# Last layer of a four-layer transformer kernel: up products in another order, one stored down product behind each, and the bias of four batches moved ahead

## The chip, the cores and the metric

The kernel runs on one core of one Trainium2 chip. The metric is the device time of one execution in microseconds (us); lower is better. TensorE does the matrix products (in the profile PE, and PEld for its weight loads), VectorE is DVE, ScalarE is ACT, GpSimd is POOL, and SyncE (SP) issues most of the DMAs.

## What is computed

The reference runs four layers one after the other on x [16, 256, 256] with context [16, 256, 256]. Each is x = x + layer(layernorm(x)): an attention whose keys are picked by an argmax, a top-2 mixture of experts, a cross attention with 16 heads of 64, and last the one that the change touches:

```python
grouped = x.reshape(b, s // 32, 32, d)          # 128 groups of 32 tokens, d = 256
logits = einsum('bntd,des->bntes', grouped, Wc) + bc + tie
perm = (logits == max over the 32 tokens)        # one token for each of 128 units (e, s)
permuted = einsum('bntd,bntes->bnesd', grouped, perm)
inner = relu(einsum('bnesd,esdf->bnesf', permuted, W1) + b1)       # f = 32
result_permuted = einsum('bnesf,esdf->bnesd', inner, W2) + b2
result = einsum('bnesd,bntes->bntd', result_permuted, perm)
```

So each of 128 units has small weights W1 [256, 32] and W2 [32, 256] of its own ("up" and "down"), applied to one picked token of each of 128 groups. b2 is added by unit and carried back to the tokens by perm.

## The kernel before, in words

Every engine has one instruction stream, written out by hand for all layers; semaphores (`w.wait_ge`) order them. The order on an engine is the order of the calls in the code, so an instruction that waits holds up all that stands behind it on its engine. The last layer consists of two parts.

**Steps** (`pe_step`, `dve_step`, `act_step`, `pool_step`, n from 0 to 19). They run over the 16 batches of 256 tokens, pipelined: at step n TensorE turns the choice of batch n-2 (L1765), computes the logits of n-1 (L1773), turns batch n (L1781) and gathers the picked tokens of n-3 (`gather`, L1799: 32 matmuls into the four banks GATHER). ACT and DVE copy the gathered tokens to `PX` (L2063, L1947). GATHER holds 64 groups after batch 7 and 64 more after batch 15. At n = 11 the four up products of the first half of the groups (batches 0 to 7, called "a" below) are made by `pe_up(…, 0, j)` (L1830, 64 matmuls, which the profile shows as 128 pairs of weight load and matmul, since one fp32 matmul is issued as two), each for a quarter j of the units, and DVE adds b1 and takes the relu (`dve_up`, L1998 and L2005).

**Tail** (`pe_tail`, `dve_tail`, `act_tail`, `pool_tail`, `sp_tail`). On TensorE:

- `pe_up(…, 1, x)`, x = 0 to 3: the up products of the second half of the groups ("b"), quarter j = PARTS[1][x]; results go to `INY[j]`, W1 comes from the buffers `WF1P`, two of which (2 and 3) lie where `RPA[1]`, `WF2P[2]` and `R2A` are placed later.
- `down_a(k)`, k = 0 to 7 (L1855, 16 matmuls, 32 pairs): down product of half a, for eight units in each half of them. DVE and ACT copy it to one of two buffers `RPA[k % 2]` (`take_a`, L2026 and L2074, two copies each). SP and POOL each store half of the buffer (512 KB each) to DRAM, `rp_scratch` (L2161, L2116). `take_a(k)` waits until the store of k-2 has ended (`rpa_free`). W2 comes in four quarters `WF2P[k // 2]` of 1024 KB; quarter 2 can only be loaded after the last up product, quarter 3 only after `down_b(1)`, and both loads (`second`, L2125) stand on SP's queue behind stores.
- `down_b(k)` (L1872, 16 matmuls, 32 pairs): the same for half b, copied to `RPB` in SBUF (L2038 and L2084). It uses the GATHER banks, and each waits until the copies of the one before it are done.
- The order was a0, up, up, up, a1, up, a2, b0, a3, b1, a4, b2, a5, b3, a6, b4, a7, b5, b6, b7. `done_a(k)` and `done_b(k)` are the counts of the semaphore s_fm that go with it.
- The last loop, i = 0 to 9: `turn_b(i)` (L1884, 16 transposes of `RPB`, to which DVE adds b2, L2048), `bias(i-2)` (L1894, 4 matmuls: perm times b2 of batch i-2 of half a), `back("b", i-1)` and `back("a", i-2)` (L1910, 8 matmuls in 16 pairs each: perm times the results). Half a is read back from `rp_scratch` into three buffers `R2A` of 1024 KB (`back_in`, L2136), the first three once all stores have ended, every further one when a buffer has been used. DVE adds the residual (`out_add`, L2020) into one of four buffers `XO`, and SP stores 256 KB to `out` (L2132). 16 outputs are stored in all.

Of the kernel before, what the change touches and what calls it, by code (L numbers as in the profile page):

```python
# [58 lines left out]
def build(nc, A, OUT):  # L59
# [1601 lines left out]
    def half(z, cc):  # L1661
# [10 lines left out]
    BC1 = mem_t("BC1", [128, 1], fp32)  # L1672
    B1 = mem_t("B1", [128, 32], fp32)
# [3 lines left out]
    GM3 = mem_t("GM3", [128, 8], fp32)  # L1677
# [5 lines left out]
    PMT = Arena(nc, w1q_at)("PMT", [128, 4096], f32r)  # L1683
    mem_t = Arena(nc, q1_at)
# [11 lines left out]
           for j, at in enumerate((q1_at + 16384, q1_at + 20480, q1_at + 8192, q1_at + 12288))]  # L1696
# [11 lines left out]
    s_pm, s_pt3, s_pb, s_ga = sem("perm"), sem("permT"), sem("permblk"), sem("gathermm")  # L1708
# [10 lines left out]
    PARTS = ((0, 1, 2, 3), (2, 3, 0, 1))  # L1719
# [39 lines left out]
    def pe_step(e, w, n):  # L1759
        def turn_choice(b):  # L1760
            w.wait_ge(s_pm, 3 * b + 3)
            w.wait_ge(s_pb, b)
            for lt in range(2):
                c0 = b * 256 + lt * 128
                m = e.transpose(PERM[:, lt * 128:lt * 128 + 128], PMT[:, c0:c0 + 128].bitcast(fp32), ident)  # L1765
            m.then_inc(s_pt3, 1)

        def logits(b):
            w.wait_ge(d_c1, 64)
            w.wait_ge(s_x3e, b + 1)  # L1770
# [63 lines left out]
    def pe_tail(e, w):  # L1834
# [6 lines left out]
        def down_a(k):  # L1841
# [18 lines left out]
        def down_b(k):  # L1860
            w.wait_ge(s_in, 20 if k else 18)
# [35 lines left out]
        def back(kind, b):  # L1897
# [36 lines left out]
    def dve_step(e, w, n):  # L1934
# [30 lines left out]

        if n == -1:
# [47 lines left out]
    def dve_tail(e, w):  # L2014
        def out_add(kind, b):
            n = returned(kind, b)
            t, m = 2 * (b + 8 * (kind == "b")), (n - 1) % 4
            w.wait_ge(s_cm2, n)
            w.wait_ge(d_x_wf2_out[m], 16 + 16 * ((n - 1) // 4))
# [9 lines left out]
        take_a(0)  # L2029
        for x in range(3):  # L2030
            dve_up(e, w, 1, x)
        take_a(1)
        dve_up(e, w, 1, 3)
        take_a(2)
        for k in range(8):
# [4 lines left out]
            if k + 3 < 8:  # L2040
# [28 lines left out]
    def act_tail(e, w):  # L2069
# [8 lines left out]
        for k in range(3):  # L2078
            take_a(k)
        for k in range(8):  # L2080
# [5 lines left out]
            if k + 3 < 8:  # L2086
# [31 lines left out]
    def sp_tail(e, w):  # L2118
# [39 lines left out]
        for k in range(8):  # L2158
# [524 lines left out]
```

## Time and profile before

| | us |
|---|---|
| median of 3 runs (lowest, highest) | 1752.61 (1751.98, 1761.69) |
| the profiled execution | 1748.76 |
| its span in the profile | 1746.9 |

The span runs from the first to the last recorded instruction; 1.86 us of the profiled execution lie outside it. All start times below are from the start of the span. Of it, TensorE is busy 94%, DVE 75%, ACT 65%, POOL 45%. The part that the change touches begins at about 1648 us (the last two gathers), the tail at 1655 us. Clock is the TensorE clock granted, as a share of 2.4 GHz. In a timeline row the text in brackets is how long the engine sat idle before it and what ended that; "issue" is idle time for which the profile shows no wait.

### The profile page before, as it was taken

What the parts mean: (1) busy time and instruction counts of PE and PEld (TensorE: products, weight loads), DVE (VectorE), ACT (ScalarE), POOL (GpSimd) and SP (SyncE); (2) the same over time, 40 slices, a digit from 0 to 9 for tenths busy, and PEclk for the clock granted to TensorE, in tenths of its full rate; (3) what the DMA queues carried; (4) which work ended last, traced back from release to release, by engine and by line L of the source; (5) the groups of instructions that cost most, each with busy time, mean ns of one, the idle gap of its engine ahead of it and who ended that gap; (6) DMA issues with size and microseconds to landing.
All of it is one profiled execution on the core that took longest, in us unless ns stands there. A gap on an engine that the chain in (4) does not pass through costs nothing.

```text
span 1746.9 us, 40702 instructions
## 1 busy us (share of the span) xinstructions
PE 1649.4 (94%) x15621; PEld 1406.7 (81%) x15621; DVE 1311.5 (75%) x2861; ACT 1129.0 (65%) x2880; POOL 791.1 (45%) x1125
## 2 busy tenths in 40 slices
PE   8899999999999999999999879999999999997768
PEld 4677776678788999999999768888888888876656
DVE  6899998452807888998888467878887888767557
ACT  2577776423347777877777467787778777764430
POOL 3344432120013334333340477888788878755300
PEclk9999999999999999999999989999999999999899
DMA  7765565156876777776777622222222222211278
GB/s 217 227 137 140 124 151 124 66 183 235 295 253 215 247 247 258 241 250 243 252 257 253 225 68 70 76 88 73 67 78 88 74 68 68 80 62 50 99 233 299
DMA packets 138770, 283.08 MB, mean 162 GB/s; under 512 B 13808, under 2 KB 89968, under 8 KB 125904
## 3 DMA queue, kind: packets, MB, share of 16 engines
q1 hardware_dynamic: 118176, 168.89, 31.9%
q0 software_dynamic: 20400, 111.59, 18.8%
q8 instruction: 124, 2.03, 0.5%
q14 instruction: 70, 0.57, 0.1%
HBM read 199.03 MB, written 81.13 MB: 160 GB/s over the span
## 4 chain that ended last, share of the span: by engine, by line
PE 69%; DVE 7%; ACT 6%; DMA 6%; POOL 6%; issue 5%; SPq 0%; POOLq 0%; DVEq 0%; ACTq 0%
PE ps L1348 12%; PE ps L1362 11%; PE ps L407 5%; PE ps L2205 5%; ACT P L220 4%; PE ps L243 4%; PE ps L2190 3%; PE ps L411 3%; PE ps L2228 3%; PE ps L500 3%; PE ps L476 3%; POOL P L233 2%; PE ps L2241 2%; PE ps L576 2%; PE ps L488 2%
## 5 line engine op out<-in xcount | busy, mean ns | idle before, releaser
L220 ACT ACTIVATE P<-ps,NM 128x256 f32<-128x256 f32 x512 | 237.6, 494 | 116.4 <-DVE NM L209 115.4
L233 POOL TENSOR_TENSOR P<-P,RS 128x1024 f32<-128x1024 f32 x128 | 244.5, 1916 | 56.3 <-DVE RS L227 55.8
L1348 PE MATMUL ps<-XRP,W1P 128*128 128x256 f32 (+1 forms) x1872 | 224.3, 279 | 3.3 <-DVE W1P L1432 3.3
L1348 PEld LDWEIGHTS ps<-XRP,W1P 128*128 128x128 f32 x1872 | 218.0, 189 | 4.0 <-DVE W1P L1432 3.6
L1362 PE MATMUL ps<-W2P,HP 128*128 128x256 f32 x1704 | 204.1, 278 | 0.0
L1362 PEld LDWEIGHTS ps<-W2P,HP 128*128 128x128 f32 x1704 | 200.2, 188 | 0.0
L642 DVE TENSOR_REDUCE NM<-ps 128x2 f32<-128x512 f32 x256 | 164.7, 685 | 28.4 <-PE ps L476 26.8
L744 ACT ACTIVATE PT<-ps 128x512 f32<-128x512 f32 x256 | 139.2, 598 | 60.1 <-PE ps L488 58.5
L209 DVE TENSOR_REDUCE NM<-ps 128x2 f32<-128x512 f32 x256 | 165.0, 684 | 3.8 <-PE ps L2190 2.4
L1281 POOL DMA_INDIRECT WE<-in_we,WIX x39 | 44.3, 1136 | 263.7 <-DVE W1P L1432 190.4
L243 PE MATMUL ps<-CST,P 128*128 128x128 f32 x1024 | 139.7, 280 | 18.0 <-ACT PT L250 16.8
L250 ACT ACTIVATE PT<-ps 128x512 f32<-128x512 f32 x256 | 143.1, 636 | 3.9 <-PE ps L243 2.0
L1392 ACT ACTIVATE HF<-ps,WE 128x256 f32<-128x256 f32 (+1 forms) x312 | 123.0, 445 | 33.1 <-PE ps L1348 29.6
L243 PEld LDWEIGHTS ps<-CST,P 128*128 128x128 f32 x1024 | 110.9, 142 | 36.2 <-issue 20.8
L1382 ACT ACTIVATE W2P<-WE 128x512 fp32r<-128x512 f32 x156 | 97.2, 623 | 53.2 <-PE ps L1362 50.7
L2205 PE MATMUL ps<-PT,V 128*64 128x256 f32 x1024 | 124.8, 385 | 1.3 <-DVE OT L2322 1.3
L2190 PEld LDWEIGHTS ps<-K,Q 64*128 64x128 f32 x1536 | 96.5, 188 | 28.2 <-issue 20.3
L1277 POOL DMA_INDIRECT XR<-xn_scratch,RIX x71 | 74.2, 1045 | 97.8 <-PE ps L1323 43.5
L220 ACT ACTIVATION_READ_ACCUMULATOR P<-ps,NM 128x1 f32 x512 | 116.1, 227 | 0.0
L1074 ACT ACTIVATE KVM<-ps 128x512 f32<-128x512 f32 x92 | 54.4, 598 | 93.2 <-PE ps L411 34.9
L2190 PE MATMUL ps<-K,Q 64*128 64x256 f32 x1536 | 109.5, 289 | 3.3 <-POOL K L2493 2.2
L2241 PE MATMUL ps<-W1O,OT 128*128 128x256 f32 x768 | 107.8, 291 | 3.5 <-DVE OT L2322 3.5
(287 smaller groups left out, 3669.6 us busy)
## 6 DMA issues: line engine op xcount, KB each, us to landing
KS<-k_scratch SPq DMA_DIRECT2D x64, 256.0 KB
V<-v_scratch SPq DMA_DIRECT2D x16, 1024.0 KB, 7.2
k_scratch<-KVM SPq DMA_DIRECT2D x52, 256.0 KB
QS<-q_scratch SPq DMA_DIRECT2D x96, 128.0 KB, 4.2
v_scratch<-KVM SPq DMA_DIRECT2D x40, 256.0 KB
ctx_scratch<-CHL SPq DMA_DIRECT2D x32, 256.0 KB, 2.7
CHR<-ctx_scratch SPq DMA_DIRECT2D x16, 512.0 KB, 4.7
ys_scratch<-YS SPq DMA_DIRECT2D x32, 256.0 KB
```

Source lines behind the costliest of these rows:

```text
L209: e.tensor_reduce(self.NM[:, u % 4, 2 * x:2 * x + 2], PS[SB1[n % 4]][:, :].rearrange("p (h j) -> p h j", h=2), AX.X, ALU.max, negate=True) ...
L220: i = e.activation(self.P[u % 4][:, c, :], PS[SB1[n % 4]][:, y * 256:y * 256 + 256], ACT.Exp, bias=self.NM[:, u % 4, c:c + 1], accum_out=s ...
L233: e.tensor_tensor(p, p, self.RS[:, u % 4, :].unsqueeze(2).to_broadcast([128, 4, 256]), ALU.mult).then_inc(self.s_pn, 1)
L243: i = e.transpose(PS[TB1[h]][:, c0:c0 + 128], self.P[u % 4][:, c, jt * 128:jt * 128 + 128], ident)
L250: e.activation(self.PT[u % 4][h][:, :], PS[TB1[h]][:, :], ACT.Copy).then_inc(self.s_tv, 1)
L642: e.tensor_reduce(NM0[b % 2][:, :, 8 * h + p], PS[SB[(2 * u + h) % 3]][:, :].rearrange("p (l j) -> p l j", l=2), AX.X, ALU.max, negate=Tru ...
L744: e.activation(PT0[u % 4][h][:, :], PS[TB[h]][:, :], ACT.Exp).then_inc(s_ex0, 1)
L1348: m = e.matmul(PS[p][:, hh * 256:hh * 256 + n], W1P[i % 2][wi][:, cc * 1024 + hc * 128:cc * 1024 + hc * 128 + 128], XRP[i % 2][xi][:, cc * ...
L1362: m = e.matmul(PS[4 + k][:, s * 256:s * 256 + 256], HP[k][hi][:, hc, s * 128:s * 128 + 128], W2P[k][wi][:, hc * 256:hc * 256 + 256], start ...
L2190: m = e.matmul(PS[SB1[(2 * u + h) % 4]][:, lt * 256:lt * 256 + 256], Q1[i][64 * h:64 * h + 64, p, lt * 128:lt * 128 + 128], K1[j][64 * h:6 ...
L2205: m = e.matmul(OB1[64 * h:64 * h + 64, c0:c1], V1[b % 2][:, jt, (2 * p + h) * 64:(2 * p + h) * 64 + 64], a1.PT[u % 4][h][:, jt * 256:jt * ...
L2241: m = e.matmul(M, OT1[b % 2][oi][:, cc, lt * 128:lt * 128 + 128], W1O[wi][:, cc, :], start=(cc == 4 * half and n == 0), stop=(not half and ...
```

## The change

1. `PARTS[1]`, the order of the quarters of the second up products, goes from (2, 3, 0, 1) to (0, 2, 3, 1). So that this is possible `INY[0]` moves to other memory, and so do the small tiles `BC1`, `B1` and `GM3`. `rpa_free` waits for the up product that read the memory under `RPA[1]`, which is now the first of the four.
2. The order on TensorE becomes up, a0, up, a1, up, a2, up, a3, b0, a4, b1, a5, b2, b3, a6, b4, a7, b5, b6, b7, and on DVE and ACT likewise; SP issues the loads of W2's quarters 2 and 3 behind the stores of a2 and a4 instead of a1 and a3.
3. The b2 bias of batches 0 to 3 leaves the last loop. Its matmuls (4 for each batch) go ahead of the gathers of batches 14 and 15 (two batches at steps n = 17 and 18), into the four banks SMALL that are free by then, and DVE adds each to the residual X with one operation of 128x512. `back("a", b)` for b < 4 then opens its bank itself.

```diff
-    assert mem_t.at <= w1q_at
+    assert mem_t.at + 4096 <= w1q_at
...
-    PARTS = ((0, 1, 2, 3), (2, 3, 0, 1))
+    PARTS = ((0, 1, 2, 3), (0, 2, 3, 1))
+    DONE_A, DONE_B = (1, 2, 3, 4, 6, 8, 11, 13), (5, 7, 9, 10, 12, 14, 15, 16)
+    BIAS_AT = {17: ((0, 0), (1, 3)), 18: ((2, 1), (3, 2))}
...
-        w.wait_ge(s_u3, 7 if k == 1 else 0)
+        w.wait_ge(s_u3, 5 if k == 1 else 0)
...
+        def bias_first(b, r):
+            M, tok = PS[SMALL[r]], 256 * b
+            w.wait_ge(s_x3e, 16 if r == 0 else 0)
+            w.wait_ge(s_pm, 48 if r == 1 else 0)
+            w.wait_ge(s_pb, 16 if r == 2 else 0)
+            w.wait_ge(s_rb, 64 if r == 3 else 0)
+            w.wait_ge(s_b2, 2)
+            for lt in range(2):
+                for j in range(2):
+                    m = e.matmul(M[:, lt * 256:lt * 256 + 256], PMT[:, tok + lt * 128:tok + lt * 128 + 128], B2S[j][:, :],
+                                 start=(lt == 0 and j == 0), stop=(j == 1), skip_group_check=True)
+            m.then_inc(s_pt3, 1)
...
+        for b, r in BIAS_AT.get(n, ()):
+            bias_first(b, r)
         if is_batch(n - 3):
             gather(n - 3)
...
-            w.wait_ge(s_in, 20 if k else 18)
+            w.wait_ge(s_in, 20 if k >= 4 else 18)
...
-        down_a(0)
-        for x in range(3):
+        for x in range(4):
             pe_up(e, w, 1, x)
-        down_a(1)
-        pe_up(e, w, 1, 3)
-        down_a(2)
+            down_a(x)
         for k in range(8):
             down_b(k)
-            if k + 3 < 8:
+            if k < 2:
+                down_a(k + 4)
+            if k in (3, 4):
                 down_a(k + 3)
...
-            if i >= 2:
+            if i >= 6:
                 bias(i - 2)
...
+        def bias_add(b, r):
+            xv = flat(X[:, 2 * b:2 * b + 2, :])
+            w.wait_ge(s_pt3, 16 + b + 1)
+            e.tensor_tensor(xv, xv, PS[SMALL[r]][:, :], ALU.add).then_inc(s_pm, 1)
...
-            if k == 1:
+            if k == 2:
                 w.wait_ge(s_u3, 8)
                 second(2)
-            elif k == 3:
+            elif k == 4:
                 w.wait_ge(s_fm, done_b(1))
                 second(3)
```

## Rows read from the trace of the kernel before

**Rows 1.** Stretches: us, then PE, PEld, DVE, ACT, POOL busy, PEclk, DMA share, GB/s.
```profile
1667.00:1672.40 5.40, 3.82 (x200) 3.02 (x200) 2.77 (x5) 1.09 (x2) 0.58 (x1) 1.00 0.11 24
1672.40:1678.00 5.60, 3.40 (x74) 2.56 (x80) 2.83 (x6) 1.08 (x2) 0.55 (x1) 1.00 0.97 236
1710.00:1742.00 32.00, 30.57 (x380) 22.00 (x378) 26.35 (x43) 0.00 (x0) 0.00 (x0) 1.00 1.03 344
1718.00:1722.00 4.00, 4.00 (x52) 2.94 (x52) 3.54 (x7) 0.00 (x0) 0.00 (x0) 1.00 0.91 273
```

**Rows 2.** Chain that ended last, 1720 us to the end, shares by line.
```profile
by line: DMA out<-XO 60.6%; DVE XO L2020 10.1%; PE ps L1884 7.0%; PE ps L1910 5.5%; PE ps L1894 1.8%; SPq L2136 1.7%; SPq L2132 1.4%; issue 1.2%; DVEq L30 0.2%
```

**Rows 3.** Timeline, the last two gathers, a copy, the first down product; then a stretch.
```profile
1649.37 1.11 PE L1799 MATMUL ps<-PB,X3P 32*128 32x128 f32 x32 [1.37 <-ACT PX L2063]
1651.97 1.97 PE L1799 MATMUL ps<-PB,X3P 32*128 32x128 f32 x32 [1.48 <-DVE PX L1947]
...
1650.53 1.29 DVE L1947 COPY PX<-ps 128x512 f32<-128x512 f32 x2 [1.83 <-PE ps L1799]
...
1655.26 2.01 PE L1855 MATMUL ps<-WF2P,INT 32*64 32x256 f32 x32 [1.31 <-DMA WF2P<-in_wf]
...
1652.00:1654.00 2.00, 1.94 (x32) 1.75 (x32) 0.01 (x1) 0.01 (x1) 0.00 (x0) 0.50 0.99 389
```

**Rows 4.** Timeline of TensorE, the second up products and what follows.
```profile
1657.20 4.00 PE L1830 MATMUL ps<-PX,WF1P 128*32 128x64 f32 x224
...
1662.90 1.99 PE L1830 MATMUL ps<-PX,WF1P 128*32 128x64 f32 x128 [1.70 <-issue]
...
1667.19 0.65 PE L1830 MATMUL ps<-PX,WF1P 128*32 128x64 f32 x32 [2.30 <-issue]
...
1671.31 0.88 PE L1830 MATMUL ps<-PX,WF1P 128*32 128x64 f32 x48 [1.38 <-issue]
...
1677.64 0.27 PE L1872 MATMUL ps<-INY,WF2P 64*128 64x128 f32 x1 [2.20 <-issue]
```

**Rows 5.** Timeline of the queues, stores and W2 loads; W2's times to landing.
```profile
1671.01 0.58 POOL L2116 DMA_DIRECT2D rp_scratch<-RPA  x1 [11.22 <-DVE RPA L2026]
...
1672.47 0.59 SPq L2125 DMA_DIRECT2D WF2P<-in_wf  x1
...
1675.58 0.55 POOL L2116 DMA_DIRECT2D rp_scratch<-RPA  x1 [3.99 <-DVE RPA L2026]
...
1682.94 0.59 SPq L2125 DMA_DIRECT2D WF2P<-in_wf  x1
...
1699.24 0.55 POOL L2116 DMA_DIRECT2D rp_scratch<-RPA  x1 [2.17 <-DVE RPA L2026]
...
DMA to landing us min/median/max: 5.3/7.0/10.7
```

**Rows 6.** Timeline of the down products.
```profile
1683.21 1.12 PE L1855 MATMUL ps<-WF2P,INT 32*64 32x256 f32 x32 [0.30 <-DMA WF2P<-in_wf]
...
1697.62 1.29 DVE L2026 COPY RPA<-ps 128x512 f32<-128x512 f32 x2 [1.03 <-DMA rp_scratch<-RPA]
...
1703.61 2.06 PE L1872 MATMUL ps<-INY,WF2P 64*128 64x128 f32 x32 [1.39 <-DVE RPB L2038]
```

**Rows 7.** The last loop: timeline, then two pieces of the chain.
```profile
1706.01 2.71 SPq L2136 DMA_DIRECT2D R2A<-rp_scratch  x3
...
1728.82 1.97 PE L1884 MATMUL ps<-CST,RPB 128*128 128x128 f32 x16
...
1733.05 1.97 PE L1884 MATMUL ps<-CST,RPB 128*128 128x128 f32 x16
...
1734.61 0.69 DVE L2020 TENSOR_TENSOR XO<-X,ps 128x512 f32<-128x512 f32 x1 [1.59 <-DMA out<-XO]
...
1741.98 1.07 PE L1910 MATMUL ps<-R2A,PMT 128*32 128x256 f32 x16 [1.43 <-DMA R2A<-rp_scratch]
...
1718.09 0.47 PE ps L1894 x4
```

More of the change, by code:

```diff
@@ L1671, in build @@
     WC1 = mem_t("WC1", [128, 2, 128], fp32)
-    BC1 = mem_t("BC1", [128, 1], fp32)
-    B1 = mem_t("B1", [128, 32], fp32)
     X3T = mem_t("X3T", [128, 2, 256], fp32)
@@ L1676, in build @@
     LT3 = mem_t("LT3", [128, 256], fp32)
-    GM3 = mem_t("GM3", [128, 8], fp32)
     x3_at = mem_t.at
     X3 = [mem_t(f"X3{i}", [128, 2, 256], fp32) for i in range(4)]
-    assert mem_t.at <= w1q_at
+    assert mem_t.at + 4096 <= w1q_at
     WF2P = [Arena(nc, x3_at)("WF2P0", [128, 8, 256], fp32)]
@@ L1683, in build @@
     PMT = Arena(nc, w1q_at)("PMT", [128, 4096], f32r)
+    mem_t = Arena(nc, attn_at + 65536 + 192)
+    BC1 = mem_t("BC1", [128, 1], fp32)
+    B1 = mem_t("B1", [128, 32], fp32)
+    GM3 = mem_t("GM3", [128, 8], fp32)
     mem_t = Arena(nc, q1_at)
@@ L1695, in build @@
     INY = [Arena(nc, at)(f"INY{j}", [128, 8, 2, 64], fp32)
-           for j, at in enumerate((q1_at + 16384, q1_at + 20480, q1_at + 8192, q1_at + 12288))]
+           for j, at in enumerate((x3_at + 8192, q1_at + 20480, q1_at + 8192, q1_at + 12288))]
     R2B = [Arena(nc, w1o_at + 8192 * i)(f"R2B{i}", [128, 8, 256], fp32) for i in range(2)]
@@ L1707, in build @@
     s_x3, s_x3p, s_x3t, s_x3e, s_lg3 = sem("x3"), sem("x3split"), sem("x3T"), sem("x3evict"), sem("logits3")
-    s_pm, s_pt3, s_pb, s_ga = sem("perm"), sem("permT"), sem("permblk"), sem("gathermm")
+    s_pm, s_pt3, s_pb, s_ga = sem("perm_biasadd"), sem("permT_biasmm"), sem("permblk"), sem("gathermm")
     s_px, s_py, s_u3, s_in, s_b2 = sem("px_act"), sem("px_dve"), sem("upmm3"), sem("inner3"), sem("b2split")
@@ L1736, in done_a @@
     def done_a(k):
-        return k + 1 if k < 3 else 2 * k - 1
+        return DONE_A[k]
     def done_b(k):
-        return 2 * k + 4 if k < 5 else k + 9
+        return DONE_B[k]
     def by_act(b):
@@ L1847, in down_a @@
             w.wait_ge(s_pb, 16)
+            w.wait_ge(s_pm, 48 + 4)
             if k:
@@ L1905, in back @@
                 w.wait_ge(s_e0, 16 + 4 * b + 4)
-                w.wait_ge(s_xo, n - 4)
+            opens = kind == "b" or b < 4
+            w.wait_ge(s_xo, n - 4 if opens else 0)
             for lt in range(2):
@@ L1910, in back @@
                     m = e.matmul(M[32 * g:32 * g + 32, lt * 256:lt * 256 + 256], PMT[:, c0:c0 + 32].bitcast(fp32),
-                                 R[:, 2 * g + lt, :], start=(kind == "b" and lt == 0), stop=True, skip_group_check=True)
+                                 R[:, 2 * g + lt, :], start=(opens and lt == 0), stop=True, skip_group_check=True)
             m.then_inc(s_cm2, 1)
-        down_a(0)
-        for x in range(3):
+        for x in range(4):
             pe_up(e, w, 1, x)
-        down_a(1)
-        pe_up(e, w, 1, 3)
-        down_a(2)
+            down_a(x)
         for k in range(8):
             down_b(k)
-            if k + 3 < 8:
+            if k < 2:
+                down_a(k + 4)
+            if k in (3, 4):
                 down_a(k + 3)
@@ L1981, in dve_step @@
             norm(n + 1)
+        for b, r in BIAS_AT.get(n, ()):
+            bias_add(b, r)
         if n == UP_AT:
@@ L2018, in out_add @@
             w.wait_ge(s_cm2, n)
+            w.wait_ge(s_pm, 48 + 4)
             w.wait_ge(d_x_wf2_out[m], 16 + 16 * ((n - 1) // 4))
@@ L2027, in take_a @@
             i.then_inc(s_e0, 1)
-        take_a(0)
-        for x in range(3):
+        for x in range(4):
             dve_up(e, w, 1, x)
-        take_a(1)
-        dve_up(e, w, 1, 3)
-        take_a(2)
+            take_a(x)
         for k in range(8):
@@ L2039, in dve_tail @@
             i.then_inc(s_e0, 1)
-            if k + 3 < 8:
+            if k < 2:
+                take_a(k + 4)
+            if k in (3, 4):
                 take_a(k + 3)
@@ L2077, in act_tail @@
         w.wait_ge(s_om, 64)
-        for k in range(3):
+        for k in range(4):
             take_a(k)
@@ L2085, in act_tail @@
             i.then_inc(s_e1, 1)
-            if k + 3 < 8:
+            if k < 2:
+                take_a(k + 4)
+            if k in (3, 4):
                 take_a(k + 3)
```

## The prediction, made before the changed kernel was run

> **What bounds the kernel now.** I read the chain of waits from its end first. In its last 27 us, 60.6% is the DMA out<-XO and 10.1% the DVE operation that feeds it; the products of TensorE have a small part [rows 2]. The stretches say why: from 1710 to 1742 us the DMA engines move 344 GB/s at a share of 1.03 [rows 1]. So the last loop has two limits close together. TensorE makes a round in 1733.05 - 1728.82 = 4.23 us without a wait until about 1737, and a round asks for one readback and two outputs, 1024 + 2 x 256 KB = 1.57 MB, which is 372 GB/s. DVE waits for a free XO at 1734.61, and TensorE for R2A at 1741.98 [rows 7]. DMA is the nearer limit.
>
> Before it, from 1655 to 1706 us, the timeline of TensorE comes next. The second up products don't run through: TensorE stops at 1661.2, 1664.9, 1670 and 1675.4 for 1.70, 2.30, 1.38 and 2.20 us, with no wait shown ("issue") [rows 4]. Counting pairs (an up product is 128, a down product 32), the stops are 128 pairs apart: 32 + 224 up to the first, then 128, then 32 + 32 + 64, then 64 + 32 + 31. So TensorE waits for its instructions in blocks of 128 pairs, and a block comes 4.29 and 4.12 us after the one before it started (1662.90, 1667.19, 1671.31), but 6.33 us (1677.64) while the DMA share is 0.97 instead of 0.11 [rows 1, 4].
>
> From 1678 on the down products alternate. b products are tied in a ring (product 2.06, copies 1.29, handing over 0.1 each, 3.45 us a round [rows 6]); the a products run beside them as long as a load or a store isn't late. a4 waited for W2's quarter 2, and the copy of a7 at 1697.62 for the store of a5 [rows 6]. The last store, issued at 1699.24, opens the readback at 1706.01 [rows 5, 7]; b7, begun at 1703.61, ends at 1705.67 and opens the last loop on TensorE. Two streams, the stores and the b products, thus reach the last loop together.
>
> **The change part by part.**
>
> *Bias ahead of the gathers.* Two batches of 4 matmuls go into each of two gaps of TensorE, 1.37 us before the gather at 1649.37 and 1.48 us before the one at 1651.97 [rows 3]. Four matmuls hold the chain 0.47 us [rows 7], two batches about 1.0 to 1.4 us with the fill: they fit, hidden by the copies to PX for which the gathers wait. DVE gets 4 x 0.69 us (the size of its XO operation [rows 7]): two in its free time before the copies of 1650.53, two behind those (they end at 1651.82) and before 1653.99. Cost 0; if the cover is short by 0.3 us each time, 0.6. On the other side, TensorE was at clock 0.50 in 1652 to 1654 (1.2 GHz) after the two gaps, and gather and first product took 1.97 and 2.01 us where a gather took 1.11 [rows 3]. With the gaps filled it may stay at 2.4 GHz: up to 0.9 us gained. I take 0 for all of it.
>
> *Up product first.* a0 began at 1655.26, when W2 had landed; the copies to PX ended at the same time (1.29 us behind the gather that ended at 1653.94 [rows 3]). The up product can start at 1655.3, so nothing is lost, and a0 comes some 3 us later. The blocks: the 16 pairs of bias have moved ahead, so the first stop falls after 240 pairs instead of 256, at pair 80 of the second up product. The block before that one starts at pair 112 of the first up product. At 4.00/224 = 17.9 ns a pair [rows 4] that is 1657.3, at a half clock up to 1658.1; I take 1657.7. The old one started at 1657.20 + 96 x 17.9 ns = 1658.9 and the next came 4.0 us later. So blocks now come at 1661.7, 1665.9, 1670.1 and 1674.3 (by 4.2), the last at 1676.4 if it takes 6.3. With 1.99/128 = 15.6 ns a pair the last up product ends at 1670.1 + 112 x 15.6 ns = 1671.8, before: 1672.45. One down product more is made by then, in time that had been a stop.
>
> *Stores.* a1 ends 48 + 32 pairs into the block of 1661.7, near 1663.6; its copy stands on DVE behind that of the up product, and the store goes at 1665.5 instead of 1671.0. a2's goes at 1670.1 instead of 1675.58 [rows 5]. a0's comes some 3 us later than before, and nobody waits for it. a3 straddles the block of 1674.3 to 1676.4; its store goes at 1676 to 1678.
>
> *W2's quarter 2.* Its load waits on SP for the last up product, as before: 1671.9 instead of 1672.47. But a4, for which it is, now stands in front of b1, and b1 waits behind it. b0 ends at 1676.7 to 1678.8 (before about 1677.9), and the load takes between 5.3 and 10.7 us, the 10.7 being this very load, beside two stores [rows 5]. In the new order only the rest of a2's store and then a3's are beside it. I take 8.5, between the median 7.0 and 10.7: it lands at 1680.4. Then a4, b1 end at 1680.4 + 0.1 + 1.12 + 2.1 = 1683.7, where b1 had ended at 1682.9. The W2 wait of a4 was there before too (0.30 us at 1683.21), but with nothing lost behind it.
>
> *From b1 to b7.* Before 22.8 us, with four a products between and two waits for stores. The floor is 6 x 3.45 = 20.7. Now three a products stand between; the stores lead by up to 5 us, so their waits mostly go. What is late next is quarter 3: it is loaded after b1 (before at 1682.94 [rows 5]), lands by the same 8.5 us at 1692.2, and a6, behind b3 (1683.7 + 2 x 3.45 = 1690.6), waits some 1.5 us with b4 behind it. 20.7 + 1.5 = 22.2 gives 1705.9, the floor 1704.4. I take 1705.5: 0.2 earlier than 1705.67. The a stream: a7 follows b4 at about 1695.7 and its store goes near 1698.0 instead of 1699.24; with the same 6.8 us to the readback, that starts at 1704.7, 1.3 earlier.
>
> *Last loop.* Four rounds lose 0.47 us each: 1.9 us on TensorE, with the 0.2 above 2.1. DMA has 8 x 1.05 + 16 x 0.26 = 12.6 MB to move and is full from 1710 on, so it only gives back the 1.3 us by which the readback is earlier, and what was not filled: 273 GB/s in 1718 to 1722 instead of the mean of 344 [rows 1] are 0.28 MB, 0.8 us. Together 2.1, so both limits allow about 2.1 us. Bounds: 0 (readback not earlier, DMA full) and 3.
>
> Sum on the profiled execution: 1748.76 - 2.1 = 1746.7. The median of the runs is 3.85 higher, 1752.61; the same difference there gives 1750.5 us.
>
> [...] The stops at multiples of 128 pairs, 1.4 to 2.3 us each, are in rows 4. [...]
>
> **The rivals.**
>
> *1. The load decides (slower).* Quarter 2 again takes 10.7 us: it lands at 1682.6 and b1 ends at 1685.9, 3.0 later than before; quarter 3 is issued as much later, so both streams arrive about 2.5 to 3 late. The last loop gives back 0.9 to 1.9. End: 1.3 later, 1753.9; with the late block of 1676.4 and the bias uncovered (0.6) up to 3 later, 1755.6. It decides from a landing after about 1682. For it speaks the 10.7 itself; against it, that one store less is in front.
>
> *2. Nothing moves.* The last loop is DMA's, 1.03 of share, and its start doesn't shift: 1752.6.
>
> *3. The stores were the limit all along.* The load takes 7.0, lands at 1678.9, b1 ends at 1682.2 and the b ring runs at its floor: b7 ends at 1702.9, 2.8 earlier, the readback starts as much earlier, and with 1.9 of the loop it is 4.7 less, 1747.9. Against it: the load of quarter 3.
>
> [...]
>
> **How the numbers follow.** My forecast (1749 to 1752) 0.50, rival 1 0.22, rival 2 0.12, rival 3 0.12, rival 4 0.04. The range takes in all terms: below, rival 4's 1746.6 with the 0.9 us of the clock and a little scatter of runs, 1745.0; above, 1755.6 with as little, 1756.0. A measurement of this kernel tells about 1% from no change, 17.5 us; no case reaches it in a stretch of 90 us whose stores, loads and products all remain: faster 0.01, same 0.98, slower 0.01.
>
> **What would show it.** Right: gaps ahead of the last two gathers filled by L1894-like matmuls with gathers no later than 1649.4 and 1652; stops 128 pairs apart between 1655 and 1677; the store of a1 near 1665.5, a2 near 1670; a4 waiting for W2 after b0, at about 1680.4; readback near 1704.7; four rounds of about 3.8 us on TensorE, but more waits of DVE on out<-XO and of TensorE on R2A at the end. Wrong: a last up product far from 1671.8, a landing after 1682 or before 1679, b7 off 1705.5 by over 1.5, or a last loop that shortens by all of 1.9 beyond its start.

## The result, and the profile after

| | before | after |
|---|---|---|
| median, us (12 runs each) | 1754.43 | 1762.59 |
| lowest and highest | 1750.04, 1762.96 | 1754.59, 1772.17 |
| profiled execution, its span | 1748.76, 1746.9 | 1764.75, 1763.0 |

The ratio is 1.0041, 95% interval 1.0023 to 1.0058: the change makes the kernel 4 to 10 us slower. A gain of 2 us had been forecast, and 1762.59 lies outside the range given. The two profiled executions differ by more (16 us) than the medians (8 us), since the one of before lies 5.7 us below its median and the one of after 2.2 us above. So single traces tell where time goes, and the ratios how much it is.

The last gathers and the bias, against [rows 3] (PE, then one DVE row, then PE):

```profile
1650.72 1.20 PE L1816 MATMUL ps<-B2S,PMT 128*128 128x256 f32 x8
1652.39 1.11 PE L1802 MATMUL ps<-PB,X3P 32*128 32x128 f32 x32 [0.47 <-issue]
1653.43 1.22 PE L1816 MATMUL ps<-B2S,PMT 128*128 128x256 f32 x8
1654.98 1.11 PE L1802 MATMUL ps<-PB,X3P 32*128 32x128 f32 x32 [0.33 <-DVE PX L1966]
...
1656.15 1.29 DVE L1966 COPY PX<-ps 128x512 f32<-128x512 f32 x2
...
1657.58 3.10 PE L1848 MATMUL ps<-PX,WF1P 128*32 128x64 f32 x113 [1.49 <-DVE PX L1966]
```
The eight bias matmuls take 1.20 and 1.22 us in the gaps, and the last gather takes 1.11 us instead of 1.97: TensorE's clock was 1.00 in 1650.0 to 1656.1, where before has 0.50 in 1652 to 1654 [rows 3]. From the start of the gather before it to its own end it is now 3.70 us, before 4.57. This part went as foreseen, or 0.9 us better. But the first up product stops after 113 pairs.

The up stage, against [rows 4]:

```profile
1662.90 0.43 PE L1848 MATMUL ps<-PX,WF1P 128*32 128x64 f32 x15 [2.22 <-issue]
...
1667.02 0.87 PE L1848 MATMUL ps<-PX,WF1P 128*32 128x64 f32 x47 [1.35 <-issue]
...
1674.76 2.33 PE L1848 MATMUL ps<-PX,WF1P 128*32 128x64 f32 x80 [5.01 <-issue]
...
1678.64 1.99 PE L1848 MATMUL ps<-PX,WF1P 128*32 128x64 f32 x128
...
1682.11 0.80 PE L1874 MATMUL ps<-WF2P,INT 32*64 32x256 f32 x17 [0.86 <-issue]
```
The stops are still at multiples of 128 pairs, and two of them are longer than before: 2.22, 1.35, 5.01 and 0.86 us. Between the last two lies a block that came without a stop, about 1678.9 by the count of pairs. The block that began to run at 1667.02 was followed by the next at 1674.76, 7.7 us later. The page of after counts engines' instructions and the packets of a queue "q8 instruction" over the span; between 1667.1 and 1672.2 that queue has no packet, and in the 0.4 us from 1672.2 it has one (last row):

```profile
PE 1652.8 (94%) x15621; PEld 1408.7 (80%) x15621; DVE 1314.1 (75%) x2865; ACT 1129.4 (64%) x2880; POOL 791.0 (45%) x1125
...
q8 instruction: 124, 2.03, 0.5%
...
q8 instruction: 1, 0.02, 14.6%
```
No view names the engine of these packets. 124 of them stand against 31242 matmuls and weight loads, 252 of these for each packet, and the stops are 128 pairs (256) apart; the other engines have 1125 to 2880 instructions. From these counts and the times I take them for TensorE's blocks. The packet started 5.2 to 5.6 us after the block of 1667.02 had begun, and 2.2 to 2.6 us ahead of the first pair of the next. The stretches, columns as in [rows 1], show what DMA did meanwhile:

```profile
1667.00:1672.30 5.30, 2.73 (x127) 2.05 (x128) 2.77 (x5) 1.09 (x2) 0.74 (x2) 1.00 0.89 212
1682.90:1692.00 9.10, 2.04 (x39) 1.85 (x38) 2.58 (x4) 2.17 (x4) 0.55 (x1) 0.81 0.95 288
1692.00:1694.00 2.00, 2.00 (x34) 0.95 (x34) 0.00 (x0) 0.00 (x0) 0.00 (x0) 0.50 0.25 102
1734.00:1738.00 4.00, 4.00 (x53) 2.90 (x51) 4.00 (x8) 0.00 (x0) 0.00 (x0) 1.00 0.69 197
```
From 1667.0 to 1672.3 the DMA engines are busy 0.89 of the time, with the stores of a0 and, from 1671, of a1. In before they were at 0.11 in 1667.0 to 1672.4 [rows 1], and the block took 4.1 us.

The queues, against [rows 5], and the down products, against [rows 6]:

```profile
1671.06 0.58 POOL L2144 DMA_DIRECT2D rp_scratch<-RPA  x1 [3.89 <-DVE RPA L2053]
...
1680.46 0.55 POOL L2144 DMA_DIRECT2D rp_scratch<-RPA  x1 [8.83 <-DVE RPA L2053]
...
1680.72 0.60 SPq L2153 DMA_DIRECT2D WF2P<-in_wf  x1
...
1696.67 0.59 SPq L2153 DMA_DIRECT2D WF2P<-in_wf  x1
...
DMA to landing us min/median/max: 5.3/8.1/11.2
```
```profile
1691.96 2.02 PE L1874 MATMUL ps<-WF2P,INT 32*64 32x256 f32 x32 [7.06 <-DMA WF2P<-in_wf]
1693.90 2.72 PE L1891 MATMUL ps<-INY,WF2P 64*128 64x128 f32 x32
...
1707.56 2.02 PE L1874 MATMUL ps<-WF2P,INT 32*64 32x256 f32 x32 [4.03 <-DMA WF2P<-in_wf]
...
1709.50 3.42 PE L1891 MATMUL ps<-INY,WF2P 64*128 64x128 f32 x32
...
1721.21 2.06 PE L1891 MATMUL ps<-INY,WF2P 64*128 64x128 f32 x32 [1.39 <-DVE RPB L2062]
```
Quarter 2 of W2 is asked for at 1680.72 (before 1672.47), 0.3 us behind the store of a2 (1680.46), and lands 11.2 us later. a4 waits 7.06 us for it with b1 behind, and starts when b1 had long been done in before (1682.9). Quarter 3 can only be asked for after b1, at 1696.67 (before 1682.94), and a6 waits 4.03 us for it with b4 behind. After each of these waits TensorE's clock is lower for a while (0.50 in 1692 to 1694 and in 1707.5 to 1709.6, 0.59 in 1709.5 to 1713), and a4 takes 2.02 us instead of 1.12 and b4 3.42 instead of 2.06. In before b1 met the same behind a stop, at clock 0.55:

```profile
1679.34 3.57 PE L1872 MATMUL ps<-INY,WF2P 64*128 64x128 f32 x32 [0.38 <-DVE RPB L2038]
```
b7 ends at 1723.27, 17.6 us later than before. The chain that ended last shows what became of the path. In before two waits for stores are its longest pieces between the up products and the last loop, in after the two loads of W2 one behind the other (start, us; the first two rows are of before):

```profile
1675.58 10.35 DMA rp_scratch<-RPA
1690.24 7.27 DMA rp_scratch<-RPA
1680.72 11.19 DMA WF2P<-in_wf
1696.67 10.85 DMA WF2P<-in_wf
```

The last loop, against [rows 2] and [rows 7]: first the chain from 1736 us to the end, then the timeline.

```profile
by line: DMA out<-XO 82.8%; DVE XO L2047 9.8%; issue 1.1%; DVEq L30 0.2%
```
```profile
1721.87 2.38 SPq L2164 DMA_DIRECT2D R2A<-rp_scratch  x3
...
1737.00 1.97 PE L1903 MATMUL ps<-CST,RPB 128*128 128x128 f32 x16
...
1740.76 1.97 PE L1903 MATMUL ps<-CST,RPB 128*128 128x128 f32 x16
...
1750.68 0.69 DVE L2047 TENSOR_TENSOR XO<-X,ps 128x512 f32<-128x512 f32 x1 [1.48 <-DMA out<-XO]
...
1758.10 1.07 PE L1930 MATMUL ps<-R2A,PMT 128*32 128x256 f32 x16 [1.68 <-DMA R2A<-rp_scratch]
```
A round of TensorE is 1740.76 - 1737.00 = 3.76 us, as worked out, and DMA out<-XO has 82.8% of the chain. From the first transpose to the end it is 38.3 us instead of 39.8.

Put together, counted from the end of the last gather (1653.9 and 1656.1 us): b0 starts 7.3 us later, b0 to b7 takes 8.1 us more, and from there it is 1.5 us less, 13.9 in all.

### The profile page after: what moved, and what is told of

It reads as the page before. It is cut to its first block, busy times and chain, and to the rows that moved or that the text cites. A ratio compares the mean times of both kernels' runs of the same rounds, so it can differ in the third digit from the quotient of the medians.

```text
span 1763.0 us, 40708 instructions
## 1 busy us (share of the span) xinstructions
PE 1652.8 (94%) x15621; PEld 1408.7 (80%) x15621; DVE 1314.1 (75%) x2865; ACT 1129.4 (64%) x2880; POOL 791.0 (45%) x1125
## 4 chain that ended last, share of the span: by engine, by line
PE 69%; DVE 8%; POOL 6%; ACT 6%; issue 6%; DMA 5%; SPq 0%; POOLq 0%; ACTq 0%; DVEq 0%
PE ps L1348 12%; PE ps L1362 11%; PE ps L407 5%; PE ps L2233 4%; ACT P L220 4%; PE ps L243 3%; PE ps L2218 3%; PE ps L411 3%; PE ps L500 3%; PE ps L2256 3%; PE ps L476 3%; POOL P L233 2%; PE ps L2269 2%; PE ps L488 2%; PE ps L576 2%
## 5 line engine op out<-in xcount | busy, mean ns | idle before, releaser
L2218 PEld LDWEIGHTS ps<-K,Q 64*128 64x128 f32 x1536 | 96.4, 188 | 28.4 <-issue 20.3
```

The lines of the kernel that those rows point to most:

```text
L2218: m = e.matmul(PS[SB1[(2 * u + h) % 4]][:, lt * 256:lt * 256 + 256], Q1[i][64 * h:64 * h + 64, p, lt * 128:lt * 128 + 128], K1[j][64 * h:6 ...
```

## The experiments

Two theories were set against each other. **L**: the loss comes from a4 and a6, which wait for their quarters of W2 in front of b1 and b4. **F**: it comes from the up stage, where blocks of instructions come late, because stores now run beside it. This table, worked out from the timeline of each kernel, is what the runs are read by (us in one profiled execution; "tail" is from the end of the last gather to the end of the span; each ratio is to runs of before on the same chip).

| kernel | last gather to end of up products | to start of b0 | b0 to b7 | first transpose to end | tail | ratio, 95% interval |
|---|---|---|---|---|---|---|
| before | 18.5 | 19.5 | 32.3 | 39.8 | 93.0 | |
| after | 24.5 | 26.8 | 40.4 | 38.3 | 106.9 | 1.0041 (1.0023, 1.0058) |
| after_again | 25.8 | 30.5 | 33.6 | 38.2 | 103.6 | 1.0049 (1.0029, 1.0070) |
| bias_only | 18.8 | 19.8 | 31.8 | 39.7 | 92.6 | 0.9997 (0.9982, 1.0012) |
| order_only | 25.0 | 29.3 | 36.9 | 39.5 | 107.0 | 1.0064 (1.0040, 1.0088) |
| a4_behind_b1 | 25.5 | 31.2 | 28.8 | 38.0 | 99.4 | 1.0010 (0.9992, 1.0027) |
| a4_ahead | 19.1 | 20.1 | 43.6 | 40.1 | 105.2 | 1.0040 (1.0018, 1.0062) |
| a_first | 24.0 | 24.8 | 28.8 | 38.1 | 93.0 | 0.9990 (0.9968, 1.0013) |
| short_stores | 20.0 | 22.9 | 33.8 | 38.3 | 96.4 | 1.0006 (0.9981, 1.0031) |
| extra_dma | 23.7 | 24.7 | 34.6 | 40.1 | 100.8 | 1.0030 (1.0006, 1.0054) |
| early_w2 | 20.2 | 21.2 | 31.4 | 38.2 | 92.1 | 1.0004 (0.9988, 1.0020) |
| early_w2_a0 | 23.0 | 24.0 | 33.6 | 38.1 | 97.1 | 1.0015 (0.9997, 1.0033) |
| a3_up_front | 19.5 | 23.5 | 29.2 | 39.4 | 93.4 | 0.9992 (0.9973, 1.0012) |
| a1_early | 18.6 | 22.6 | 29.5 | 39.0 | 92.5 | 0.9998 (0.9977, 1.0019) |

"To start of b0" counts from the last gather too, and between b7 and the first transpose lie 1.4 us in every kernel. In the eight traces with a tail over 96 us the tail lies 1.5 to 6.7 us further above that of before than the ratio gives (13.9 against 7.2 us in after). No run shows why.

### bias_only: the third part of the change alone

The changed kernel with the order of the weights, of the products, of their copies on DVE and ScalarE and of SP's loads put back (PE's part of it shown):

```diff
-    PARTS = ((0, 1, 2, 3), (0, 2, 3, 1))
+    PARTS = ((0, 1, 2, 3), (2, 3, 0, 1))
...
-        for x in range(4):
+        down_a(0)
+        for x in range(3):
             pe_up(e, w, 1, x)
-            down_a(x)
+        down_a(1)
+        pe_up(e, w, 1, 3)
+        down_a(2)
         for k in range(8):
             down_b(k)
-            if k < 2:
-                down_a(k + 4)
-            if k in (3, 4):
+            if k + 3 < 8:
                 down_a(k + 3)
```

> The kernel before with only the bias of batches 0 to 3 moved ahead (order of the products and queue positions as before). Theory L (the loss comes from a4 and a6, which wait for their quarters of W2 in front of b1 and b4): no loss here, time 0 to 2 us below before, a4 again behind b1. Theory F (the 16 pairs that moved ahead shift the blocks of instructions, so that a block is waited for inside the first up product): a stop of about 2 us inside the first up product here too, the last up product 2 us later than before, time 0 to 2 us above before. In both the last loop has four shorter rounds (3.76 instead of 4.23 us).

Ratio 0.9997: neither gain nor loss. The stop in the first up product, which F expected here too, isn't there:

```profile
1666.90 3.15 PE L1848 MATMUL ps<-PX,WF1P 128*32 128x64 f32 x209
...
1676.84 0.87 PE L1848 MATMUL ps<-PX,WF1P 128*32 128x64 f32 x47 [3.67 <-issue]
```
209 pairs run through, and with the 32 of a0 the first stop comes at 241. The block 128 pairs earlier begins 113 pairs behind the last gather, just where the first stop of after is, and here it was there in time. So the part that F put on the 16 shifted pairs falls. The last loop is 39.7 us, no shorter than before: its rounds are shorter (3.76 us instead of 4.23) and the waits for DMA longer (DVE for out<-XO 6.8 us instead of 5.0, TensorE for R2A 2.1 instead of 1.4).

### order_only: the first two parts alone

```diff
-    BIAS_AT = {17: ((0, 0), (1, 3)), 18: ((2, 1), (3, 2))}
+    BIAS_AT = {}
...
-            if i >= 6:
+            if i >= 2:
                 bias(i - 2)
```

> The changed kernel with the bias of all batches left in the last loop, as before. Theory L: slower than before by all that the change lost, 7 to 9 us, with a4 and a6 waiting 4 to 7 us for W2. Theory F: the stop inside the first up product is gone and with it some 2 us; 4 to 6 us slower than before.

Ratio 1.0064: the order holds the whole loss. Its up stage is as long as that of after (25.0 us), and a stop of 2.01 us behind the first up product is still there, which F had expected to be gone. L had expected both a4 and a6 to wait; only a6 did, 6.09 us. Quarter 2 landed 5.7 us after it was asked for.

### a4_behind_b1

```diff
         for k in range(8):
             down_b(k)
-            if k < 2:
-                down_a(k + 4)
-            if k in (3, 4):
+            if 1 <= k <= 4:
                 down_a(k + 3)
...
-            elif k == 4:
+            elif k == 3:
```

> The changed kernel with b1 ahead of a4, so that the order from there on is b0, b1, a4, b2, a5, b3, a6, b4, a7, b5, b6, b7, and the load of quarter 3 behind the store of a3. Theory L: b1 follows b0 at once, quarter 3 is asked for about 8 us earlier, both waits that held b products shrink, and the time comes back to within 3 us of before. Theory F (late blocks of instructions make the up products and the load of quarter 2 late, and everything follows): b1 gains, but a4 and b2 are as late as in the changed kernel; 4 to 6 us above before.

Ratio 1.0010, against 1.0041: within 3 us of before, as L says, and under the 4 to 6 us that F alone expected (though the interval reaches 4.7 us). b0 to b7 is 28.8 us, shorter than in before and in the three traces with the order of after (40.4, 33.6, 36.9). In its parts L came out less well. Quarter 2 landed after 6.3 us, so that a4 would hardly have waited in front of b1 either. Quarter 3 was asked for 38.4 us after the last gather instead of 40.6, 2 us earlier and not 8, but it landed after 6.2 us instead of 10.9, and no product waits for it.

The up stage stays at 25.5 us, and b0 starts 11.7 us later than in before. The b products take back 3.5 of that and the last loop 1.8. In this trace 6.4 us remain, where the ratio gives 1.8: the two don't agree, and why is open.

### a4_ahead: before, with a4 put in front of b1 and a5 in front of b2

```diff
         for k in range(8):
             down_b(k)
-            if k + 3 < 8:
-                down_a(k + 3)
+            for x in ((3, 4), (5,), (), (6,), (7,), (), (), ())[k]:
+                down_a(x)
...
-            elif k == 3:
+            elif k == 4:
```

> The kernel before with nothing but a4 put in front of b1 (and, as in the changed kernel, b2 and b3 next to each other, and quarter 3 loaded behind the store of a4): a0, up, up, up, a1, up, a2, b0, a3, a4, b1, a5, b2, b3, a6, b4, a7, b5, b6, b7. Theory L (a4's and a6's waits in front of b products are a loss of their own): the up stage as before (quarter 2 asked for some 18.5 us after the last gather), b0 to b7 5 to 8 us longer, ratio 1.003 to 1.005. Theory F (the loss is in the up stage, whose late blocks make quarter 2 late): within 0.001 of before.

The load of quarter 3 goes behind the store of a4, as in the changed kernel. Ratio 1.0040, as much as the whole change, with an up stage of 19.1 us. L's mechanism alone is enough for the measured loss:

```profile
1687.54 1.12 PE L1856 MATMUL ps<-WF2P,INT 32*64 32x256 f32 x32
1693.37 2.01 PE L1856 MATMUL ps<-WF2P,INT 32*64 32x256 f32 x32 [4.71 <-DMA WF2P<-in_wf]
...
1711.16 2.01 PE L1856 MATMUL ps<-WF2P,INT 32*64 32x256 f32 x32 [6.39 <-DMA WF2P<-in_wf]
```
a4 waits 4.71 us for quarter 2 and a6 6.39 us for quarter 3, though quarter 2 was asked for as early as in before. b0 to b7 is 11.3 us longer, where 5 to 8 had been expected.

### short_stores: after, with stores of a0 to a2 cut to a quarter

```diff
+            cut = slice(0, 16 if k < 3 else 64)
-            e.dma_start(rpd_part(k, 0), rpa_half(k, 0)).then_inc(d_ks_rp[k % 4], 16)
+            e.dma_start(rpd_part(k, 0)[cut], rpa_half(k, 0)[cut]).then_inc(d_ks_rp[k % 4], 16)
```

> The changed kernel, but the stores of a0, a1 and a2 carry a quarter of their bytes (the rest of that memory is filled from other data long before, so the output is not the layer's in those places). Theory F: with little for DMA to do beside the up products, every block comes 4.1 us after the one before, the stop of 5 us in the third up product shrinks to about 2, and quarter 2 is asked for 20 us after the last gather instead of 24.6. Theory L adds: quarter 2 lands within 6 to 8 us instead of 11.2. If the stops stay as long, stores are not what makes the blocks late.

Shown is SP's half of the store; POOL's is cut likewise, and the rest of that memory is filled by copies at 1591 to 1595 us, long before the tail. The up stage is 20.0 us instead of 24.5 and 25.8, and the stop of 5.01 us is gone:

```profile
1681.86 1.77 PE L1848 MATMUL ps<-PX,WF1P 128*32 128x64 f32 x112 [0.96 <-issue]
...
1685.76 0.80 PE L1874 MATMUL ps<-WF2P,INT 32*64 32x256 f32 x17 [1.52 <-issue]
...
1689.89 1.12 PE L1874 MATMUL ps<-WF2P,INT 32*64 32x256 f32 x32 [1.33 <-DMA WF2P<-in_wf]
```
a4 waits 1.33 us instead of 7.06; quarter 2, asked for at 1683.69, is there after 6.2 us. So the stores both make the blocks late and hold up quarter 2. The stop in the first up product (2.42 us) stays: no store runs there yet (SP issues the first at 1674.34; the DMA share is 0.15 in 1667.9 to 1670.3). a6 still waits 4.40 us, and the ratio is 1.0006 even so. How that is divided between the blocks and quarter 2 isn't shown. By the code the copies to RPA wait for these stores too, but of such waits the traces show 0.3 us here and none in after.

### extra_dma: before, with 2 MB of useless copies beside the up products

```diff
+            if k == 0:
+                for x in range(2):
+                    e.dma_start(kd[x], kd[2 + x]).then_inc(d_w0_w1, 16)
             if k == 1:
                 w.wait_ge(s_u3, 8)
                 second(2)
```

> The kernel before with two copies of 1 MB each from DRAM to DRAM (data that nobody needs any more) issued by SP behind the store of a0, so that the DMA engines are busy beside the up products; nothing else is changed. Theory F (the blocks of instructions of TensorE come late because DMA is busy): stops of 3 to 5 us where before has 1.4 to 2.3, quarter 2 asked for 22 to 25 us after the last gather instead of 18.5, and a time 3 to 6 us above before. If blocks don't depend on DMA traffic: 18.5 to 19.2 us as in the three kernels with the order of before.

Ratio 1.0030, and the up stage 23.7 us. The order of the products is that of before, only DMA is busier (the last row is a stretch, its columns as in [rows 1]):

```profile
1664.61 1.99 PE L1830 MATMUL ps<-PX,WF1P 128*32 128x64 f32 x128 [1.78 <-issue]
1674.38 1.08 PE L1830 MATMUL ps<-PX,WF1P 128*32 128x64 f32 x32 [7.78 <-issue]
...
1664.60:1674.40 9.80, 2.01 (x131) 1.85 (x131) 1.57 (x3) 0.00 (x0) 0.00 (x0) 0.79 0.72 265
```
The stop is 7.78 us where before has 2.30, and the two blocks start 9.8 us apart. With short_stores, that DMA traffic makes blocks late is shown from both sides. What it costs is not shown by this ratio alone: quarter 2 was late too, and a4 waited 6.13 us for it (0.30 in before).

### a_first: a4_behind_b1 with each a product ahead of its up product

```diff
         for x in range(4):
-            pe_up(e, w, 1, x)
             down_a(x)
+            pe_up(e, w, 1, x)
```

> a4_behind_b1 with each a product ahead of its up product instead of behind it: a0, up, a1, up, a2, up, a3, up, b0, b1, a4, b2 and on. If the first stop (2 to 3.5 us in the first up product wherever an up product opens the tail) hangs on what opens the tail, it is gone, and the up stage is 2 to 3 us shorter than in a4_behind_b1 (quarter 2 asked for 22 to 23 us after the last gather instead of 25.6). If it hangs on the loads of W2's quarters 0 and 1 or on the shifted blocks, it stays. The later stops stay long in both cases if stores make blocks late.

```profile
1660.37 3.64 PE L1848 MATMUL ps<-PX,WF1P 128*32 128x64 f32 x128
...
1675.21 1.43 PE L1874 MATMUL ps<-WF2P,INT 32*64 32x256 f32 x17 [2.62 <-issue]
```
The first up product runs its 128 pairs without the stop of 2 to 3.5 us (3.64 us, at a clock of 0.50), so the stop hangs on what opens the tail. It is there in all six traces (of five kernels) in which an up product does and in none of the eight in which a0 does. The later stops remain long (2.62 us inside a3), and the up stage is only 1.5 us shorter, 24.0. Ratio 0.9990, not to be told from before.

### early_w2 and early_w2_a0: quarters 2 and 3 in memory that is free earlier

early_w2, against the changed kernel, in part (early_w2_a0 has a0 ahead of the first up product; the rest is the same):

```diff
-    WF2P += [Arena(nc, at)(f"WF2P{i + 1}", [128, 8, 256], fp32) for i, at in enumerate((q1_at, ot1_at + 8192))]
-    WF2P.append(WF2P[0])
+    WF2P += [Arena(nc, at)(f"WF2P{i + 1}", [128, 8, 256], fp32) for i, at in enumerate((q1_at, q1_at + 16384, ot1_at + 8192))]
...
-    PARTS = ((0, 1, 2, 3), (0, 2, 3, 1))
+    PARTS = ((0, 1, 2, 3), (3, 2, 0, 1))
...
-        for x in range(4):
-            pe_up(e, w, 1, x)
-            down_a(x)
+        pe_up(e, w, 1, 0)
+        down_a(0)
+        pe_up(e, w, 1, 1)
+        pe_up(e, w, 1, 2)
+        down_a(1)
+        pe_up(e, w, 1, 3)
+        down_a(2)
...
         second(1)
+        w.wait_ge(s_u3, 5)
+        second(2)
```

> Quarters 2 and 3 of W2 get memory that is free earlier: the order of the up products is 3, 2, 0, 1, quarter 2 is loaded after the first of them and quarter 3 after the last. The order on TensorE is up, a0, up, up, a1, up, a2, b0, a3, b1, a4, b2 and on as before; the bias is moved ahead. Theory L: no a product waits for W2, the b products run at about 3.5 to 4 us a round, and the time is 3 to 6 us below before. Theory F: the load of quarter 2 now lies beside the up products, whose blocks of instructions come 2 us later each; at best as before, up to 4 us above.

> early_w2 with a0 opening the tail, as before. If what opens the tail decides the first stop, the up stage is 2 us shorter than in early_w2 and the time 2 to 4 us below before, ratio 0.998 to 0.999; if the loads beside the up products take it back, as early_w2, 1.000.

1.0004 and 1.0015: behind b0 no a product waits for W2 any more, and nothing is won, as F had expected and against L's 3 to 6 us. The load now lies beside the up products. With a0 ahead, the up stage is not 2 us shorter but 2.8 longer (23.0 against 20.2). In early_w2_a0 a block comes late beside the load and the store of a0 and, later, a copy waits for a store:

```profile
1678.39 1.50 PE L1847 MATMUL ps<-PX,WF1P 128*32 128x64 f32 x47 [5.59 <-issue]
...
1699.33 1.29 DVE L2054 COPY RPA<-ps 128x512 f32<-128x512 f32 x2 [6.73 <-DMA rp_scratch<-RPA]
...
1700.67 2.01 PE L1873 MATMUL ps<-WF2P,INT 32*64 32x256 f32 x32 [5.96 <-DVE RPA L2054]
```
The 5.96 us of PE are the wait for the DVE copy of the a product before, and that copy had itself waited 6.73 us for a store of RPA.

### a3_up_front and a1_early: the up stage of before with the b stage of a4_behind_b1

a3_up_front, against a4_behind_b1 (a1_early has the order a0, up, a1, up, up, up, a2, a3 instead; the rest is the same):

```diff
-        for x in range(4):
-            pe_up(e, w, 1, x)
-            down_a(x)
+        down_a(0)
+        pe_up(e, w, 1, 0)
+        pe_up(e, w, 1, 1)
+        pe_up(e, w, 1, 2)
+        down_a(1)
+        pe_up(e, w, 1, 3)
+        down_a(2)
+        down_a(3)
...
-            if k == 2:
+            if k == 1:
                 w.wait_ge(s_u3, 8)
```

> The up stage of before (a0, up, up, up, a1, up, a2), then a3 ahead of b0 and a4 behind b1: a3, b0, b1, a4, b2, a5, b3, a6, b4, a7, b5, b6, b7; bias moved ahead. Both theories together: quarter 2 asked for 18.5 to 19.2 us after the last gather, b0 to b7 in 29 to 31 us instead of 32.3, last loop 1 us shorter: 2 to 4 us below before, ratio 0.998 to 0.999. If the wait of a3's copy for the store of a1 holds the copy of b0, ratio 1.000.

> As a3_up_front, but a1 already behind the first up product: a0, up, a1, up, up, up, a2, a3, b0, b1, a4 and on. Two stores beside the up products instead of one. Theory F: blocks somewhat later, quarter 2 at 19 to 21.5 us; a3's copy doesn't wait. The time lies between a3_up_front and a_first (0.999).

0.9992 and 0.9998, where both theories together had expected 0.998 to 0.999. Both keep a short up stage (19.5 and 18.6) and a short b0 to b7 (29.2 and 29.5), but b0 starts 23.5 and 22.6 us after the last gather instead of 19.5, since a3 and its wait of 1.9 us for a2's copy stand in front. What b0 to b7 gains is spent there. No version that was run beats before beyond its interval.

### after_again

> The changed kernel once more, for a second trace, since the landing of W2's quarters and the blocks of instructions vary between executions. If both terms belong to the order and not to one execution: quarter 2 asked for 24 to 26 us after the last gather, a4 and a6 waiting 4 to 7 us for W2, b0 to b7 in 36 to 42 us, ratio 1.003 to 1.006.

Ratio 1.0049, as expected, but by another way:

```profile
1678.03 0.55 POOL L2144 DMA_DIRECT2D rp_scratch<-RPA  x1 [5.24 <-DVE RPA L2053]
...
1682.80 0.59 SPq L2153 DMA_DIRECT2D WF2P<-in_wf  x1
...
1691.19 1.82 PE L1874 MATMUL ps<-WF2P,INT 32*64 32x256 f32 x32
...
1705.98 1.73 PE L1874 MATMUL ps<-WF2P,INT 32*64 32x256 f32 x32 [4.09 <-DMA WF2P<-in_wf]
```
The up stage was worse (25.8 us), and with another late block inside a3 b0 only started at 30.5. Quarter 2 was asked for 4.8 us behind the store of a2 instead of 0.3, and landed after 5.9 us instead of 11.2; the DMA engines moved 1.22 MB in that time, and 2.95 MB in the 11.2 us of after. a4 didn't wait at all, and b0 to b7 is 33.6 us, less than the 36 expected. a6 waited 4.09 us.

So the wait of 7.06 us that a4 shows in the first trace doesn't come with the order each time: it is missing in the second trace and in order_only. In these traces it goes with how close in front of the load the store of a2 was issued (0.3 us against 4.8 and 4.6), which in after came late behind the stop of 5.01 us. What all three traces have is an up stage of 24.5 to 25.8 us, a b0 that starts 7.3 to 11.0 us later than in before, and a6 waiting 4.03 to 6.09 us with b4 behind it.

## Why the prediction was wrong

**Bias ahead of the gathers: right.** Hidden, and the 0.9 us at a clock of 1.00, which I had bounded but not taken, came. In the time it can't be told from nothing (bias_only, 0.9997, interval from 0.9982).

**Up product first: the step that failed.** "blocks now come at 1661.7, 1665.9, 1670.1 and 1674.3 (by 4.2)". I had read in [rows 1, 4] that a block takes 4.1 us with DMA idle and 6.3 with DMA busy, and then used 4.2 for every block, in a change that moves two stores beside those very blocks; the 6.3 was only granted to the last. By the same count of pairs the measured ones are 1667.02, 1674.76, about 1678.9 and 1682.11. The block before them, for which I took 1657.7 and no stop, came at 1662.90. The last up product ended at 1680.6 instead of 1671.8. Of the 8.8 us 2.2 are the later start of the tail in this execution, 3.0 the block of 1662.90 and 3.5 the one of 1674.76, 7.7 us behind its predecessor instead of 4.2. short_stores has an up stage 4.5 to 5.8 us shorter than the two traces of after. By the stop in the first up product the term "so nothing is lost" of opening with an up product was wrong too.

**W2's quarter 2: right in place, wrong in size.** I wrote that a4 "now stands in front of b1, and b1 waits behind it", and took 8.5 us for the load, 1680.4. It was asked for 8.8 us later than worked out and took 11.2. I took a value below the 10.7 that this same load had shown, because one store less would be in front; with every store also later, that didn't hold. By the 10.7 the rival would have been the forecast. The load is not always that long, though: with the order of after it took 11.2, 5.9 and 5.7 us in three traces. I also left b1 at its full speed of 2.1 us behind the wait, though in before it took 3.57.

**From b1 to b7: mis-sized.** 21.8 us (1683.7 to 1705.5) were given; measured 1696.6 to 1723.3, 26.7. a6 waited 4.03 us, not 1.5, and a6 and b4 then took 0.9 and 1.4 us more, at a clock of 0.50 and 0.59. No term stood for that. Together these are the 4.9 us. Added up, the span came out 18.2 us over the 1744.8 forecast for it (1746.9 - 2.1): 12.9 of them by the end of b1, 4.9 from there to the end of b7, and 0.4 behind it.

**Stores and last loop.** The stores of a1 and a2 went at 1671.1 and 1680.5, not at 1665.5 and 1670.1. Four rounds of 3.76 us came as worked out, and the loop shortened by 1.5 us against the 1.9 of TensorE alone. That readback and outputs would be filled better held only in part: in 1734 to 1738 the DMA engines moved only 197 GB/s; the fourth readback was asked for at 1734.26, 12.4 us behind the first (10.7 in before).

**The rivals.** Rival 1 (the load decides) named a right mechanism, and a4_ahead shows that it is enough by itself for the measured ratio. Its price, 1.3 to 3 us, was 16 to 37% of the measured 8.2: it carried one late block at its upper end, and neither the others nor quarter 3's longer wait nor the clock. Rival 2 failed, since the first readback moved by 15.9 us, 13.7 counted from the last gather. Rival 3 failed: b7 ended at 1723.27, not 1702.9. Rival 4's 1746.6, on which the lower end of the range (1745.0) stands, takes an up stage without stops. No run shows that term: the stops of 128 pairs came back in every trace, of 0.6 us (bias_only) to 7.8 us (extra_dma, where only DMA traffic was added), and the up stage took 18.5 to 25.8 us.

The chance of 0.98 for "within 1%" held: 0.41%. The range didn't: its upper end was 0.2% above the median shown, narrower than the terms themselves allowed once 6.3 us a block and 10.7 us a load are added.

**What stays open.** Why the first stop comes when an up product opens the tail. In the eight traces where a0 opens, the next packet on the instruction queue goes out between 0.3 us before and 1.5 us after the end of the last gather; in the six where an up product does, 4.2 to 4.8 us after it. bias_only and after differ in this (1.0 to 1.3 and 4.5 to 4.8 us), though the next block begins 113 pairs behind the gather in both and both ask for W2's first quarters 3.3 us before its end. So neither the place of the block nor that load explains it; what does isn't shown by any run. Open too is how the loss of 7 to 9 us is divided between the late blocks and the loads: a4_ahead loses as much with a short up stage, a_first loses nothing with a long one, and the parts don't add up.

## What to carry to other kernels

When work is moved so that transfers run beside a stage of many small instructions, cost the stage with the durations it shows while DMA is busy, for instructions too, and not with those of the quiet stage. Before an instruction that waits for a load is moved ahead of one that doesn't, price the load at the longest landing that the trace shows for it as well as at its median, and follow who can only start the next load afterwards. A gain in a ring (28.8 instead of 32.3 us here) counts only from where the ring starts.

## What the runs showed that was not expected

- A block of 128 pairs of small matmuls is run through in 2.0 us (1.99 at a clock of 1.00, from 1662.90 in before), but the next one came 4.1 us after the one before with the DMA engines 0.01 busy (1662.90 to 1667.02 in after), 6.3 and 7.7 with them 0.97 and 0.89 busy, and 9.8 with two useless copies. The least in any trace, by the count of pairs, is 3.1 (short_stores). At the four stops of before a packet on the instruction queue starts at 1659.9, 1664.8, 1668.4 and 1675.2, 2.3 to 3.0 us ahead of the first pair (1662.90, 1667.19, 1671.31 and 1677.64). In the up stage TensorE was held by these stops, and not only by its own speed: in after it was busy 11.98 of the 21.0 us from 1661.0.
- A load of 1024 KB took 5.2 us at the least (early_w2). Quarter 2 took 5.9 us where the DMA engines moved 1.22 MB meanwhile (after_again) and 11.2 us where they moved 2.95 MB (after); the longest load was quarter 3 of a4_ahead, 13.1 us, with 3.13 MB moved.
- But for the bias products, buffer places and the filling copies of short_stores, the code ahead of the tail is the same in all kernels, and the last gather ended between 1653.9 and 1663.6 us in the fourteen traces. That scatter of 10 us in the earlier layers is larger than the effect, and only the ratios over many runs show it.
